# Attention 0's product with the values: probabilities stationary, result by queries, no transposes and no copy

## What is computed

```python
x = x + _L0_attn_ref(_layernorm(x, axis=-1), L0_attn_Wq, L0_attn_Wk, L0_attn_Wv, L0_attn_Wo)
x = x + _L0_xattn_ref(ctx_1024, _layernorm(x, axis=-1), L0_xattn_in_proj_w, ...)
x = x + _L0_ffn_ref(...)
x = x + _L1_attn_ref(...)
x = x + _L1_xattn_ref(ctx_1024, ...)
x = x + _L1_ffn_ref(...)
```

```python
def step(state, inp):
    d, b, c, u = inp
    dA = jnp.exp(d[..., None] * A)
    state = state * dA + (d * u)[..., None] * b[:, None, :]
    y = jnp.einsum('bdn,bn->bd', state, c)
    return (state, y)
```

## Time and profile before

| | |
|---|---|
| median of 3 runs | 966.31 us (966.12 to 970.98) |
| the profiled execution | 971.37 us, its span 969.6 us |
| busy in the span | PE 807.5 us (83%), DVE 722.8 (75%), ACT 478.7 (49%), POOL 213.1 (22%) |
| PE's mean granted clock | 0.918 of 2.4 GHz |
| attention 0's units | from 109.8 us (first scores) to 219.8 us (last `at0`) |

### The profile page before, as it was taken

The page is one execution under the profiler, slowest core; times in us unless marked ns, Lnnn a source line. Parts: engine busy times, 40 slices in busy tenths (PEclk is TensorE's granted clock), DMA queues, the critical chain, the costliest instruction groups (busy, mean ns, idle before and its releaser), DMA issues.

```text
span 969.6 us, 11879 instructions
## 1 busy us (share of the span) xinstructions
PE 807.5 (83%) x3952; PEld 575.7 (59%) x3952; DVE 722.8 (75%) x1090; ACT 478.7 (49%) x990; POOL 213.1 (22%) x155
## 2 busy tenths in 40 slices
PE   6752679897599996789988879889883799999997
PEld 2331445555443563566666656656762579999996
DVE  4879999899866986899899788869937734444443
ACT  1743546460326302567657556646772435444442
POOL 1000000002220022011101111201003356666663
PEclk9685779899799998899999999999996899999999
DMA  4304122234020212011110111111200044434431
GB/s 163 129 26 160 65 108 97 78 109 186 42 93 0 66 44 87 22 45 47 40 61 28 44 46 43 44 45 43 68 1 0 1 158 151 141 130 147 146 130 44
DMA packets 24208, 74.60 MB, mean 77 GB/s; under 512 B 3120, under 2 KB 5696, under 8 KB 23776
## 3 DMA queue, kind: packets, MB, share of 16 engines
q1 hardware_dynamic: 23776, 71.51, 20.8%
q10 hardware_dynamic: 384, 2.49, 0.8%
HBM read 72.55 MB, written 1.44 MB: 76 GB/s over the span
## 4 chain that ended last, share of the span: by engine, by line
PE 46%; DVE 29%; issue 11%; ACT 11%; POOL 2%; DMA 0%; POOLq 0%; DVEq 0%; ACTq 0%; SPq 0%
DVE hS L899 9%; PE ps L1535 6%; PE ps L1649 6%; PE ps L1650 6%; PE ps L1651 6%; DVE hS L891 4%; PE ps L1496 4%; PE ps L1614 3%; PE ps L1515 2%; PE ps L1602 2%; ACT dA L531 2%; PE ps L1300 2%; DVE arena L1167 2%; DVE arena L1148 1%; PE ps L1593 1%
## 5 line engine op out<-in xcount | busy, mean ns | idle before, releaser
L899 DVE TENSOR_TENSOR_SCAN hS<-dA,hS 128x1024 f32<-128x1024 f32 x64 | 146.3, 2286 | 28.6 <-ACT dA L531 27.5
L1273 DVE SCALAR_TENSOR_TENSOR arena<-ps,arena 128x1024 f32<-128x1024 f32 x32 | 39.2, 1224 | 102.1 <-ACT arena L771 93.1
L1300 PE MATMUL ps<-ident,hS 128*128 128x128 f32 x512 | 71.3, 288 | 38.2 <-DVE hS L902 38.1
L1300 PEld LDWEIGHTS ps<-ident,hS 128*128 128x128 f32 x512 | 60.9, 148 | 66.1 <-DVE hS L902 46.6
L1535 PE MATMUL ps<-WB,hT 128*128 128x512 f32 x192 | 88.6, 606 | 3.8 <-DVE arena L1148 2.0
L531 ACT ACTIVATE dA<-DEL,negA 128x510 f32<-128x510 f32 x128 | 84.8, 718 | 5.4 <-DVE hS L899 5.0
L420 POOL TENSOR_TENSOR MHl<-arena,MHh 128x1024 fp32r<-128x1024 f32 x34 | 81.8, 2405 | 16.8 <-ACT MHh L774 16.8
L1649 PE MATMUL ps<-Wh,MHh 128*128 128x256 f32 x272 | 77.8, 286 | 5.9 <-POOL MHl L420 5.9
L902 DVE TENSOR_TENSOR hS<-hS,BCb 128x1024 f32<-128x1024 f32 x64 | 78.4, 1225 | 2.2
L891 DVE TENSOR_TENSOR hS<-DU,BCb 128x1024 f32<-128x1024 f32 x64 | 77.7, 1214 | 0.1
L1650 PE MATMUL ps<-Wl,MHh 128*128 128x256 f32 x272 | 77.6, 285 | 0.0
(11 more groups left out here) (220 smaller groups left out, 1884.1 us busy)
## 6 DMA issues: line engine op xcount, KB each, us to landing
BCb<-bc_dram SPq DMA_DIRECT2D x64, 512.0 KB, 3.6
arena<-gate_dram SPq DMA_DIRECT2D x32, 512.0 KB, 3.7
WB<-in_we SPq DMA_DIRECT2D x34, 256.0 KB, 2.7
WB<-in_wqkv SPq DMA_DIRECT2D x1, 3072.0 KB, 12.7
WA<-in_wo ACTq DMA_DIRECT2D x1, 2048.0 KB, 7.9
WA<-in_ffn SPq DMA_DIRECT2D x1, 1408.0 KB, 8.1
pkb<-in_pk SPq DMA_DIRECT2D x2, 698.0 KB, 4.8
X<-in_x SPq DMA_DIRECT2D x1, 1024.0 KB, 7.4
```

The costliest lines, as they stand in the source:

```text
L899: v.tensor_tensor_scan(f(h), f(a), f(h), 0.0, ALU.mult, ALU.add).then_inc(s["scan_done"], 1)
L1300: last = mm(ps[:, ACC_BANK + j // 2, 256 * (j % 2) + P * d:256 * (j % 2) + P * d + P], src[:, d, P * j:P * j + P], ident[:], start=(first ...
```

## The change

The two operands of `pv0` trade places. The probabilities of a block of 128 queries are now stationary (128 rows, 128 columns), and the 33 columns of `V0` stream. Each unit has 2 blocks of queries, 2 heads and 2 blocks of keys: 8 matmuls instead of 2. The result comes out with queries on the partitions, 4 groups of 33 columns, in bank 4 or 5 by turns, where `at0` reads it. `pv0_copy`, `pv0_tr`, `O0` and their semaphores go. `pv0(u)` now waits for `at0(u-2)` instead of `pv0_copy(u-1)`. The scan is as it was.

```diff
-            def pv0_copy(u):
-                act.wait_ge(s["pv0_mm"], u + 1)
-                if u:
-                    act.wait_ge(s["pv0_tr"], u)
-                sc.copy(O0, ps[0:D0 + 1, 4, :]).then_inc(s["pv0_copied"], 1)
...
             def at0(u):
-                dve.wait_ge(s["pv0_tr"], u + 1)
+                dve.wait_ge(s["pv0_mm"], u + 1)
...
-                o = ps[:, 5, 0:4 * (D0 + 1)].rearrange("p (h d) -> p h d", d=D0 + 1)
+                o = ps[:, 4 + u % 2, 0:4 * (D0 + 1)].rearrange("p (h d) -> p h d", d=D0 + 1)
...
                 pe.wait_ge(s["s0_exp"], 2 * (u + 1))
                 pe.wait_ge(s["v0_ready"], KV0)
-                if u:
-                    pe.wait_ge(s["pv0_copied"], u)
-                for kb_ in range(2):
-                    last = mm(ps[0:D0 + 1, 4, :], V0[:, 2 * b + kb_, D0 * g:D0 * g + D0 + 1], PT0[u % 2][:, :, kb_, :],
-                              start=(kb_ == 0), stop=(kb_ == 1))
-                last.then_inc(s["pv0_mm"], 1)
-
-            def pv0_tr(u):
-
-                pe.wait_ge(s["pv0_copied"], u + 1)
-                if u:
-                    pe.wait_ge(s["at0_ready"], u)
+                if u >= 2:
+                    pe.wait_ge(s["at0_ready"], u - 1)
                 for t in range(2):
                     for r in range(2):
                         c = (2 * t + r) * (D0 + 1)
-                        last = tr(ps[:, 5, c:c + D0 + 1], O0[:, S * r + P * t:S * r + P * t + P], ident[0:D0 + 1, 0:D0 + 1])
-                last.then_inc(s["pv0_tr"], 1)
+                        for kb_ in range(2):
+                            last = mm(ps[:, 4 + u % 2, c:c + D0 + 1], PT0[u % 2][:, r, kb_, P * t:P * t + P],
+                                      V0[:, 2 * b + kb_, D0 * g:D0 * g + D0 + 1], start=(t == 0 and r == 0 and kb_ == 0),
+                                      stop=(kb_ == 1), skip_group_check=True)
+                last.then_inc(s["pv0_mm"], 1)
```

More of the change, by code:

```diff
@@ L178, in build @@
         rden0 = sb("rden0", [P, 4])
-        O0 = tabs[0:D0 + 1, :, :, :].rearrange("p a b c -> p (a b c)")[:, 0:2 * S]
         aT0 = hT
@@ L254, in build @@
             ln_mv ln_rstd ln_h ln_tr_mm ln_tr_act ln_tr_dve qkv0_mm qkv0_copied rope0_cos rope0_sin rope0_add rope0_mean rope0_rot rope0_sq rope0_rs rope0_done v0_ready k4_ready tr0_mm tr0_copied
-            s0_mm s0_tanh s0_exp pv0_mm pv0_copied pv0_tr at0_den at0_ready a_tr_mm a_tr_act a_tr_dve o0_mm x_new fsc_ready gate_tanh gate_h gate_mm gate_t nega_exp nega_ready pt0_fill
+            s0_mm s0_tanh s0_exp pv0_mm at0_den at0_ready a_tr_mm a_tr_act a_tr_dve o0_mm x_new fsc_ready gate_tanh gate_h gate_mm gate_t nega_exp nega_ready pt0_fill
             f_mm f_tanh f_hid fd_mm wdn_ready w1_mean w1_centered tabs_ready job_mm job_sq job_rot job_sum job_rstd job_add job_rope
@@ L619, in _ @@
                 sc.activation(pt[:, :, 1, P:S], TH0[u % 2][:, :, W0:W0 + P], ACT.Exp, scale=SOFTCAP).then_inc(s["s0_exp"], 1)
-                if u:
-                    pv0_copy(u - 1)
-                    if u - 1 == A_TR_UNIT:
-                        a_tr_copy(0)
+                if u - 1 == A_TR_UNIT:
+                    a_tr_copy(0)
                 steps_to(AT0_AT[u] + 1)
-            pv0_copy(UNITS0 - 1)
             steps_to(LAYER_STEPS - 1)
@@ L1444, in _ @@
                     s0(u + 1)
-                if u:
-                    pv0_tr(u - 1)
                 if u == A_TR_UNIT + 1:
@@ L1452, in _ @@
                 acc_to(AT0_AT[u] - 2)
-            pv0_tr(UNITS0 - 1)
             def o0(hf):
```

## The result

The changed kernel takes 1011.32 us (median of 4, 1003.26 to 1012.68), the kernel before beside it 968.64 (966.12 to 971.19): ratio 1.0406, 95% interval 1.0366 to 1.0446. It is 4% slower. The profiled execution's span is 1009.4 us where it was 969.6. The kernel before's runs fall into two groups (of 25 beside experiments 1 to 4, 16 took 965 to 969 us and 9 took 971 to 974), and its profiled execution, 971.37 us, is of the upper one, so the spans differ by 39.8 us where the medians differ by 42.7.

What follows compares the result with a forecast made beforehand. DVE was taken as the bound, PE 1% behind. At half clock PE's 8.62 us rounds put the last at0 38.9 us later; with the work behind it, +42 us on 966.3 gave 1008 us, range 982 to 1026.

Steps and rivals of the forecast that it cites:

- Which clock: PE in attention 0's units: clock falls to 0.50 and stays until o0 after the last unit; likeliest case, 72%.
- the falls in the first units: PE's clock in attention 0's first units: expected to fall there once the change removes the long product L1410.
- The price of a record: PE's short product: 16 records a unit at 0.11 us (full clock) or 0.21 (half), so 1.76 or 3.36 us.
- the transpose L1422: Lower bound for a product record, 0.14 us at low clock; rival with cheap loads: round 7.50, total 991 us, 8%.
- The sum: Attention 0's units to the second transposes: 14 PE rounds of 8.62 us, last at0 at 258.6, in all +42 us.
- The place of DVE's wait: DVE's steps in attention 0's units: idle 3 to 3.5 us each, at ssm_dbu for acc, none at at0.
- the clock that holds: Rival, 10%: PE keeps clock 1.00, round 4.64 us, DVE stays the bound and waits less: -3.4 us, 963.
- Two readings of the earlier trace: PE before unit 1: low-clock mix from 127.20 to 134.10 us, then nothing but L1410 until 137.50, then clock 1.00.
- The rule on loads: PE's product: load of 128 columns priced 107 ns whatever the clock, 1.7 us a unit at 1.2 GHz; unused in total.

Runs made afterwards that it cites:

- experiment 1: Changed kernel with each of the product's 8 matmuls a unit streaming 128 columns instead of 33: 967.05 us, ratio 0.9973 to the kernel before.
- Experiment 2: Changed kernel with the long stream back (values stationary, 2 matmuls of 512 columns), still without copy and transposes: 968.57 us, ratio 1.0011 to the kernel before.
- experiment 3: Changed kernel with the score matmuls on all 128 rows of the array instead of the head's 32: 965.45 us, ratio 0.9964 to the kernel before.
- experiment 4: Changed kernel with each of the product's matmuls streaming 64 columns instead of 33: 996.44 us, ratio 1.0292 to the kernel before.
- experiment 6: Changed kernel with the old long product added ahead of the short one, its result overwritten: 982.41 us, ratio 1.0156 to the kernel before.
- experiment 7: Changed kernel with each of the product's matmuls streaming 96 columns instead of 33: 967.91 us, ratio 1.0015 to the kernel before.
- experiment 5: Changed kernel with half of the short product left out, 8 records a unit instead of 16: 984.59 us, ratio 1.0178 to the kernel before.

## Why the prediction was right

- **Which clock.** This was the step that decided, and it held: PEclk 0.50 from 130 to 250 us. Forecast was that the clock returns with `o0` after the last unit, and it did: `o0(0)` took 4.87 us (259.92 to 264.79, "some 5" in the sum), and the stretch 250 to 270 has 0.68. Experiments 1, 3, 4, 6 and 7 show that the clock is the cause of the loss, and experiment 5 that PE's round then sets the pace. What it is in PE's work that brings the clock back is open: more columns (1, 7), a long stream (6) and wider scores (3) each did. One word of the forecast was off: the falls in the first units, at about 113 us and in the gap before 127 us, are those of the kernel before; what is new is that the clock did not return.
- **The price of a record.** Taken: 0.21 us at low and 0.11 at full clock, from L1603. Measured: 3.44 / 16 = 0.215 and 0.111. The nearer row was L1603 and not the transpose L1422, whose 0.14 would have given 991. That the load sets this time shows in the wider streams: at full clock 96 columns take 0.116 us a record and 128 take 0.118.
- **The sum.** The round was forecast at 8.62 us and is 8.68; the last `at0` at 258.6 and ends at 259.0; DVE's wait at the second transposes 3.2 and is 2.52. The sum +42 us stands against 1011.32 - 968.64 = 42.7, an agreement that is in part luck: the ratio's interval is 4 us wide on either side, and between the two profiled executions, on whose rows the sum rests, the loss is 39.8 us. After the second transposes' copy the changed kernel is 41.9 us behind; 1.2 of these come back by 314 us in DVE's shorter waits for the convolution, the next copy and ACT, and 0.9 later on, which I did not follow.
- **The place of DVE's wait** was wrong: I named `ssm_dbu` waiting for `acc`, and no waits of `at0`. The waits are in `at0`, for the product. `acc(10+u)` stands behind `pv0(u)` in PE's order, but step 13+u asks only for `acc(9+u)`, so the product comes last. The number is the same.
- **The 3.4 us of the clock that holds** were too much to claim. Experiment 2, which is that case, measured 1.0011 (0.9992 to 1.0030); its trace has the 2.36 us of them. The wait for `a_tr`, of which I gave back 1 us, stayed at 2.06 in experiment 1.
- **Two readings of the earlier trace rows** were a little short: L1410 begins at 133.57 us, within the stretch to 134.10, and at 137.13 `acc` begins, within the stretch of "nothing but L1410". Nothing in the sum hangs on it.
- **The rule on loads** of the Trainium skill (TensorE: Matmul & The Clock Gate, LDWEIGHTS (loading the stationary operand)) gives, by its formula, 107 ns for 128 columns, and names no clock; that it holds at either was my reading. The figure agrees with 0.111 us a record at full clock. At 1.2 GHz the trace has 0.215, so the cost of these f32 records does follow the clock, against the estimate of 1.7 us a unit that I worked out from it.

## What to carry to other kernels

When the short side of a product is made the stream, ask first what the long stream did for the clock: a round of 4.7 us at 2.4 GHz (an estimate: experiment 6's 6.50 less its long product, 1.83), under the 5.14 of the bounding engine, was 8.68 at 1.2 GHz, 69% over it. Judge it by what PE did before the clock's falls and rises in the trace of before, not by PE's busy share, which was 100% from 130 to 170 us in the bad case and in the good one. If the load bounds a record, stream up to its time: 96 or 128 columns cost little more than 33 (1.89 us instead of 1.78 for 16 records) and took back the 4% here.

## What the runs showed of the hardware

- With the same matmuls and columns, the scores on 128 instead of 32 rows of the array, the granted clock was 1.00 instead of 0.50 from 130 to 170 us (experiment 3).
- A PE that is busy all the time can be kept at 1.2 GHz: 20.00 of 20 us busy at 0.50 from 130 to 150 us in the changed kernel.
- Records of an f32 matmul with 128 loaded columns take 0.111 us at full clock with 33 streamed columns and 0.118 with 128 (experiments 3 and 1); with 33 columns at 1.2 GHz, 0.215.
- Scores on 32 rows take longer than on 128. In the changed kernel one head's scores took, at full clock,

```profile
109.16 0.30 PE L1386 MATMUL ps<-mask,identb 128*128 128x320 bf16 x1 [1.35 <-ACT arena L595]
...
110.12 0.31 PE L1386 MATMUL ps<-mask,identb 128*128 128x320 bf16 x1
```

110.12 - 109.16 = 0.96 us; in experiment 3 they took 144.21 - 143.53 = 0.68 us for the same columns. Of the 0.28 us between them, 0.19 lie in the two f32 matmuls (0.43 and 0.31 us against 0.33 and 0.22, start to start) and 0.09 between the start of the mask's matmul, which is the same in both, and the next start; whether changing from 128 to 32 rows has a part in it was not tried.
- Added work on the bounding engine can shorten a kernel: 29 us less with 2 useless matmuls a unit (experiment 6).
